# A token tower on one core: five small moves around the layer norms of group 0 and the last group's transposes

## The reference, cut to what matters

```python
# 1. token field: three convolutions over the one-hot ids give a gate, four Gaussians times cosines a basis
h = gelu(conv1d(onehot, w1, b1, 3)); h = gelu(conv1d(h, w2, b2, 2))
ctx = sigmoid(conv1d(h, w3, b3, 1))[:, 0, :]
amps = emb[ids] * ctx[:, :, None]
for s in range(4):
    z = (positions - center) / (abs_w * width[s] + 1e-5)
    basis += exp(-0.5 * z * z) * cos(phase + 2 * pi * z) * amp_scale * scale_weights[s] ** 2
h = einsum('bsp,bsd->bpd', basis, amps)
# 2. state space layer over a layer norm: h += Re(C . conv(A^t, B_bar . norm(h)))
h = h + attn(layernorm(h))
# 3. mixture of 8 experts over a layer norm, only the expert of the largest gate counts
xf = layernorm(h); H = gelu(xf @ W1 + b1); probs = softmax(H @ Wg + bg)
out = sum over e of where(argmax == e, probs[:, e] * (H @ Wd[e] + bd[e]), 0)
# 4. result
h = h + out
```

## Time and profile before

| | |
|---|---|
| median of 3 executions | 112.52 us (112.3 to 113.85) |
| profiled execution, its own time | 112.29 us |
| span of its trace, first to last instruction | 110.5 us |
| what lies around the span | 1.79 us |
| mean granted TensorE clock | 0.990 |
| PE busy | 100.0 us (90%) |
| DVE busy | 89.0 us (81%) |
| ACT busy | 70.8 us (64%) |
| POOL busy | 52.9 us (48%) |

### The profile page before, as it was taken

One profiled execution on the slowest core, in us unless ns is written; L12 is line 12 of the kernel. 1 busy time (PEld: TensorE's weight loads), 2 busy tenths in 40 slices (PEclk: granted clock), 3 DMA queues, 4 the chain that ended last, 5 costly groups with the idle time before them and its releaser, 6 DMA issues.

```text
span 110.5 us, 2010 instructions
## 1 busy us (share of the span) xinstructions
PE 100.0 (90%) x717; PEld 64.4 (58%) x723; DVE 89.0 (81%) x230; ACT 70.8 (64%) x126; POOL 52.9 (48%) x101
## 2 busy tenths in 40 slices
PE   5989999999999798789899999999999799999930
PEld 2356785364334476247666677976777476667610
DVE  0369999999969949999998799498999926498871
ACT  4604599999999999999779349156746606431000
POOL 7799999898986008007329254544005000000940
PEclk9999999999999999999999999999999999999995
DMA  3999700000000100000000000000000000000142
GB/s 90 264 244 407 270 0 0 3 0 0 6 0 3 5 1 0 0 0 6 0 0 0 0 0 6 0 0 0 0 3 6 0 0 0 0 0 0 33 98 59
DMA packets 4297, 4.15 MB, mean 38 GB/s; under 512 B 3264, under 2 KB 3520, under 8 KB 4160
## 3 DMA queue, kind: packets, MB, share of 16 engines
q1 hardware_dynamic: 4144, 3.92, 12.5%
q10 hardware_dynamic: 144, 0.12, 0.4%
HBM read 3.50 MB, written 0.52 MB: 36 GB/s over the span
## 4 chain that ended last, share of the span: by engine, by line
PE 44%; ACT 38%; DVE 5%; DMA 4%; issue 3%; POOL 2%; ACTq 0%
PE pair L1079 17%; ACT wave L475 8%; PE bank L1041 7%; ACT bell L465 7%; ACT bell L469 5%; ACT L424 5%; DMA ids<-x 4%; PE hid_pair L1052 3%; PE pair L950 3%; ACT angle L513 3%; ACT h L459 2%; PE hid_pair L1062 2%; ACT dist L454 2%; PE pair L920 2%; PE pair L1086 2%
## 5 line engine op out<-in xcount | busy, mean ns | idle before, releaser
L378 POOL TENSOR_SCALAR var_eps<-mean_var 128x4 f32<-128x4 f32 x8 | 3.7, 458 | 31.0 <-DVE mean_var L746 30.9
L818 DVE COPY_PREDICATED pair<-later,pair 128x256 f32<-128x256 int32 (+3 forms) x30 | 12.3, 410 | 5.9 <-PE pair L1079 5.2
L920 PE MATMUL pair<-warm 128*128 128x512 bf16 x49 | 12.4, 379 | 0.5 <-issue 0.5
L731 DVE SCALAR_TENSOR_TENSOR bell<-bell,scale_w,wave 128x512 f32<-128x512 f32 x16 | 11.0, 754 | 1.1 <-ACT wave L475 1.1
L1079 PE MATMUL pair<-wd_high,H_high 128*128 128x512 f32 x32 | 10.8, 418 | 0.0
L920 PE MATMUL hid_pair<-warm 128*128 128x512 bf16 x28 | 8.9, 474 | 1.5 <-POOL warm L297 1.3
L394 POOL TENSOR_TENSOR angle<-picked,prob 128x256 f32<-128x256 f32 x3 | 1.8, 613 | 17.2 <-DVE prob L842 17.2
L1079 PE MATMUL pair<-wd_low,H_high 128*128 128x512 f32 x32 | 10.0, 394 | 0.0
L520 ACT ACTIVATE bell<-hid_pair,sm 128x512 f32<-128x512 f32 x8 | 5.0, 680 | 7.2 <-PE hid_pair L1052 7.2
L674 DVE TENSOR_TENSOR wave<-dist,inv_width 128x2048 f32<-128x2048 f32 x4 | 9.1, 2298 | 0.0
L964 PE MATMUL pair<-h,w_sb 128*64 128x512 f32 x40 | 9.0, 597 | 0.0
(11 more groups left out here) (166 smaller groups left out, 228.4 us busy)
## 6 DMA issues: line engine op xcount, KB each, us to landing
ids<-x SPq DMA_DIRECT2D x2, 512.0 KB, 5.7
posb<-positions SPq DMA_DIRECT2D x1, 768.0 KB, 8.0
wd_sb<-wd SPq DMA_DIRECT2D x1, 512.0 KB, 9.2
out<-angle SPq DMA_DIRECT2D x4, 128.0 KB, 2.0
st_sb<-state SPq DMA_DIRECT2D x1, 328.0 KB, 8.3
w_sb<-w SPq DMA_DIRECT2D x1, 256.0 KB, 6.6
posb<-positions SPq DMA_DIRECT2D x1, 256.0 KB, 6.6
w_sb<-w SPq DMA_DIRECT2D x1, 160.0 KB, 8.0
```

What stands on the lines that cost most here:

```text
L731: ins = dve.scalar_tensor_tensor(out=bell[:, g, part], in0=bell[:, g, part], scalar=scale_w[:, s:s + 1], in1=wave[:, g, part], op0=ALU.mul ...
L818: return dve.copy_predicated(held[:, :, 0:n, 0, 0:D], repeat(later[:, g, 2 * h + rows.start:2 * h + rows.stop, first:first + n], 3, D), he ...
L920: pe.matmul(bank[free], warm[:, 0:P], warm[:, :], start=True, stop=True)
```

## The change

- TensorE: the first `keep_warm` has 17 matmuls and not 14.
- TensorE: `turn(1, 3)` now stands behind `logits_back(2, 4)` and `experts_high(1, 1)`.
- ScalarE: `upright_out(0)` stands ahead of `load_gelu()`, and `transposed_out(0, 0)` ahead of `square(3)`.
- VectorE: `driven(0)`, `input_gain()`, `scan(0)` and `turn_back(0)` now stand ahead of `moments(0, 1)`; before, `input_gain()` and `moments(0, 1)` came first.
- VectorE and GpSimd: for g = 0 of both norms the addition of EPS is one more instruction at the end of VectorE's `moments`, and GpSimd's `inv_std` begins with the power.
- GpSimd: `inv_std(1, 0)` stands ahead of `inv_std(0, 2)`; before, it came behind it.

```diff
@@ GpSimd: inv_std
                 pool.wait_ge(s_mv[n], g + 1)
-                link(pool.tensor_scalar(var_eps[:, n, g, :], mean_var[:, n, g, :, 1], EPS, None, ALU.add))
                 if g == 0:
                     pool.tensor_tensor(rstd[:, n, g, :], var_eps[:, n, g, :], minus_half[:, 0:GB],
                                        ALU.pow).then_inc(s_rstd[n], 1)
                 else:
+                    link(pool.tensor_scalar(var_eps[:, n, g, :], mean_var[:, n, g, :, 1], EPS, None, ALU.add))
@@ GpSimd: the list
             inv_std(0, 1)
+            inv_std(1, 0)
             inv_std(0, 2)
-            inv_std(1, 0)
             inv_std(0, 3)
@@ ScalarE: the list
             field_out(0)
+            upright_out(0)
             load_gelu()
-            upright_out(0)
             conv2_out(1)
...
             context_out(1)
+            transposed_out(0, 0)
             square(3)
-            transposed_out(0, 0)
             gaussian(3)
@@ VectorE: moments
                     ins = dve.bn_aggr(mean_var[:, n, g, b, :], stats[:, n, g, b, :])
+                if g == 0:
+                    link(ins)
+                    ins = dve.tensor_scalar(var_eps[:, n, g, :], mean_var[:, n, g, :, 1], EPS, None, ALU.add)
                 ins.then_inc(s_mv[n], 1)
@@ VectorE: the list
             product(2)
+            driven(0)
             input_gain()
-            moments(0, 1)
-            driven(0)
             scan(0)
             turn_back(0)
+            moments(0, 1)
             product(3)
@@ TensorE
-            keep_warm(14, 7)
+            keep_warm(17, 7)
...
             experts_low(1, 0)
-            turn(1, 3)
             logits_back(2, 4)
             experts_high(1, 1)
+            turn(1, 3)
             experts_low(1, 1)
```

## The result

The changed kernel took 119.49 us in the median of four executions (118.09, 118.92, 120.06, 120.38) against 112.5 us. The ratio is 1.053 with a 95% interval of 1.0475 to 1.0586. The profiled execution took 118.09 us, with a span of 116.3: 5.8 us more than the profiled one of before.

The account below looks back on a forecast made before the run. The chain of waits ran on ScalarE to about 53 us, then on TensorE to the end. Profiled 112.29 + 6.7 (both orders' losses and +0.92) - 0.57 (turn(1, 3)) = 118.4 us; range 114.9 to 120.9 us.

Parts of the forecast that it names:

- the two late moments: On VectorE: moments(0, 1) ending at 54.25 us, not about 50.25, and moments(1, 0) at 61.93, not 58.58.
- the two waits behind them: TensorE idle about 3 us ahead of turn(0, 1) and again ahead of turn(0, 2), waiting for normalise.
- The front, +0.35: Start of the kernel: three more warming matmuls take 0.65 us, 0.30 of it free; ScalarE's list 0 to 0.35 us later.
- upright_out(0), +0.57: ScalarE, group 0: it waits for two transposes that the table load had covered, +0.57 us; with the front +0.92.
- EPS on VectorE: Group 0: GpSimd's power begins 1.3 us sooner, VectorE takes some 0.2 us more; nothing on the path.
- transposed_out(0, 0): ScalarE ahead of square(3): copy at 46.67 us, cosine(3) ending near 54.3 us; nothing on the path.
- VectorE's order: First loss: late moments(0, 1) delay inv_std(0, 1), normalise(0, 1) and turn(0, 1), which goes from 55.6 to 59.0 us (+3.4).
- GpSimd's order: Second loss: inv_std(1, 0) first puts normalise(0, 2) at 65.85 us, not 59.15: +6.7 us, first loss and +0.92 included.
- turn(1, 3), -0.57: TensorE near the end: the 0.57 us wait for normalise(1, 3) goes when the transposes come later.
- The falling clock: Rival, 18%: TensorE's clock falls to its lower level in the second idle time, costing 2.2 us; sum 120.6 us.

Follow-up runs that it names:

- one execution above: Profiled execution (113.34 us) of the kernel before with only 17 warming matmuls at the front, not 14; median of twelve 112.56 us, ratio 1.001.
- with the clock held at 1.00: The changed kernel with 28 more warming matmuls where TensorE stood idle (3, 11 and 14): 117.79 us, ratio 1.047.

## Why the prediction was right, point by point

The forecast was 118.4 us, the profiled execution took 118.09, and the median of four, 119.49, lies in the range. The path is the forecast one: the two late moments and the two waits behind them. That the numbers agree within 0.3 us is partly luck. The sum had no term for the clock, and without a fallen clock the changed kernel takes 117.6 to 117.8 us: the sum was 0.6 to 0.8 us too high for what it counted, and the falling clock, which it left out, made up most of that in the profiled execution and more than that in the other three. One of the prediction's own signs of being wrong, a falling clock, did come.

- *The front, +0.35.* Free in the profiled execution: its warming matmuls took 5.28 us for 17, and the ids landed 0.3 us later (an idle time of 0.73 us stood ahead of the lookup). The price was mis-sized: I took the matmuls at full speed. At 0.43 us each the three take up to 1.3 us, and in one execution above the first lookup came 1.0 us later.
- *upright_out(0), +0.57.* Right: 0.53 us of idle time, and a ratio of 1.005 alone. Together with the ids, product(2) stood at +0.82 against the forecast +0.92. That this idle time has a second price, the 0.66 us ahead of tap(1) on TensorE, is missing in the prediction.
- *EPS on VectorE.* Right: the power began 1.17 us sooner, at 41.33 us, and an idle time of 1.23 us ahead of gates(1) covered both changes.
- *transposed_out(0, 0).* Right that it is off the path, 0.9 us off in time. TensorE's turn(0, 0) ran at the lower clock until 47.53 us, so ScalarE idled 1.39 us for it and copied at 47.57; cosine(3) ended at 55.29 us for the forecast 54.3, and product(3) waited 0.22 us for it.
- *VectorE's order.* Right in size and place. Turn(0, 1) was forecast at 59.0 us and stood at 58.67. inv_std(0, 1) beside product(3) took 2.92 us from 54.23, for the forecast 3.2; its negation of four elements alone took 0.63 us. One announced sign didn't come: ScalarE waited 1.54 us for the offset of group 1 and not over 2, since its own list ran late behind turn(0, 0); with the clock held at 1.00 it waited 2.76. TensorE idled 2.53 us ahead of turn(0, 1), for about 3. Without the fallen clock this order costs 2.1 us (114.66 us).
- *GpSimd's order.* Right. The power and inv_std(0, 2) took 4.34 us, from 61.57 to 65.91, for the forecast 3.9, as the addition met the scan (1.14 us) and the offset met turn_back (0.72). Turn(0, 2) was forecast at 67.3 us and stood at 67.42; with the clock held at 1.00 the scan came earlier against the addition, which then took 0.71 us, and turn(0, 2) stood at 66.87. Without the fallen clock this order costs 3.1 us (115.70).
- *Adding up.* 2.1 and 3.1 are 5.2 us, and the rest came out at nothing; the changed kernel with its idle time filled has 5.2 (117.79 less 112.57). By the spans of the profiled executions the same three are 2.4, 3.5 and 5.3 us, so the sum holds to about 0.6 us and no closer.
- *turn(1, 3), -0.57.* Right in mechanism; it gave 0.8 us alone.
- *The falling clock.* This rival was set too low at 18%, and it was not a case of its own but something that comes on top, in some executions more than in others. I let it fall in the second idle time only. In the changed kernel it fell already around turn(0, 0), after idle times of 0.59 and 0.66 us, and behind the first long one; the second, shortened by the slow clock itself, passed without a fall. Behind a single idle time of 2.9 or 3.4 us a fall cost about 2 us.

Still open is what makes the clock fall near turn(0, 0) in one execution and not in another. The orders are not needed for it: it fell there in the profiled executions of the changed kernel, of the one with GpSimd's swap undone and of upright_out(0) alone, and not in those with VectorE's order undone or both orders undone. All five have the same 0.65 or 0.66 us of idle time ahead of tap(1), which upright_out(0) brings in. In none of the profiled executions without it did the clock fall there, nor in the one where three matmuls filled it. Three of five is a hint and no proof, and no run was made to test it.

## What to carry to other kernels

An instruction moved behind others on one engine must be followed through every list in which its readers stand: here the moments were on no chain, but GpSimd, ScalarE's copy of the next group and TensorE's transposes stood behind them in turn. Two producers on one engine should stand in the order in which their inputs arrive; GpSimd's swap alone, one line, cost 3.1 us. And a long idle time of TensorE can cost more than its length, since what follows may run at half the clock: filling it with unread matmuls gave 2 us back where nothing else had changed. Short ones can do it too, as the execution of upright_out(0) alone shows, and a fall only costs where TensorE is the one that is waited for.

## What the runs showed of the hardware

- TensorE's granted clock went to 0.54 over the 6.5 us behind an idle time of 2.87 us, which is close to the lower of its two levels (1.2 of 2.4 GHz); the same 32 matmuls took 3.30 us and not 1.97. With the idle time filled, at the same place, they took 1.97. This is the rule of the Trainium skill (TensorE: Matmul & The Clock Gate, HAM oscillation) that idle gaps bring the throttle back, and the trace agrees, though the gap here was shorter than those that the page speaks of. What I had not expected is that it differs from execution to execution of one kernel, and so makes the spread (115.89 us at a clock of 0.999, 117.4 to 118.2 at 0.96 to 0.985).
- A GpSimd instruction of four elements takes 0.23 us undisturbed, 0.63 beside VectorE's product and 1.14 to 1.23 when it meets the scan.
- The granted clock was also 0.50 between 9 and 12 us behind an idle time of 0.72 us, in the profiled execution of upright_out(0) alone; in that of the changed kernel it stayed at 1.00 there behind one of 0.73 us.
- At the front the same 17 warming matmuls took 5.28 us in one execution and 6.79 in another, so a fixed count of them is no fixed time.
